# Expert weights prepared by ScalarE and VectorE beside the sampled scores, and VectorE's order in the recurrence changed

## The reference

```python
h = tok(x)                                        # splice, project, bias
u = layernorm(h)                                  # L0 attention: a complex linear recurrence
Bu = einsum(u, gamma * (B_re + 1j*B_im))
hs = scan(lambda s, b: s * lam + b, Bu)           # lam = exp(-exp(nu) + 1j*exp(theta)), 256 states
h += real(einsum(hs, C)) + einsum(u, D)
u = layernorm(h)                                  # L0 experts: 16, hidden 512, top 2
logits = u @ gate.T; top2; w = softmax(top2)
y_mean[e] = mean over e's tokens of silu(u @ w1[e].T), times w2[e]
h += sum over the 2 chosen of w * y_mean[e]
u = layernorm(h)                                  # L1 attention: 8 heads of 16, L = 166
q, k, v = u @ Wq, u @ Wk, u @ Wv
M = max - mean over 38 sampled keys of q . k      # "sampled scores"
top 25 queries by M attend to all keys, the others get mean(v)
h += out @ Wo
u = layernorm(h)                                  # L1 experts: 64, hidden 256, top 42
h += sum over e of comb[e] * (gelu(u @ w1[e] + b1[e]) @ w2[e] + b2[e])
```

## Time and profile before

| | us |
|---|---|
| median of 3 runs (2061.93 to 2066.79) | 2064.61 |
| the profiled execution | 2067.39 |
| its span (first to last instruction) | 2065.7 |
| recurrence, from the first outputs to the last routed group | 94 to 228 |
| last rows sent, PE idle | 228 to 283.3 |
| first experts, tiles | 283.3 to 397.7 |
| first experts, means and outputs | 397.7 to 429 |
| third norm, and start of the sampled scores | 429 to 465.9 |
| sampled scores, 16 chunks | 465.9 to 583.7 |
| attention of the chosen queries | 583.7 to 717 |
| fourth norm, routing and second experts | 717 to 2065.7 |

### The profile page before, as it was taken

The page is one execution under the profiler, slowest core; times in us unless marked ns, Lnnn a source line. Parts: engine busy times, 40 slices in busy tenths (PEclk is TensorE's granted clock), DMA queues, the critical chain, the costliest instruction groups (busy, mean ns, idle before and its releaser), DMA issues.

```text
span 2065.7 us, 50535 instructions
## 1 busy us (share of the span) xinstructions
PE 1870.1 (91%) x17038; PEld 1349.7 (65%) x17038; DVE 1676.4 (81%) x4833; ACT 1378.0 (67%) x2149; POOL 1455.0 (70%) x1098
## 2 busy tenths in 40 slices
PE   7887436789989978999999999999999999999998
PEld 5555213456669855777777777777777777777776
DVE  5887736555678788899999999999999999999998
ACT  4134525424435545888888888888888888888886
POOL 2216679559800032888888888888888888888887
PEclk9998768789989965999999999999999999999999
DMA  3011289523200010000000200000100000000000
GB/s 93 21 35 63 81 246 257 124 67 94 90 1 1 22 63 1 2 2 0 0 0 3 82 2 0 0 0 35 49 1 0 0 0 2 2 10 11 10 11 19
DMA packets 64334, 77.56 MB, mean 38 GB/s; under 512 B 38932, under 2 KB 47028, under 8 KB 62132
## 3 DMA queue, kind: packets, MB, share of 16 engines
q1 hardware_dynamic: 61364, 70.08, 11.7%
q0 software_dynamic: 2816, 5.45, 0.8%
HBM read 42.97 MB, written 24.08 MB: 32 GB/s over the span
## 4 chain that ended last, share of the span: by engine, by line
PE 58%; DVE 3%; issue 2%; ACT 1%; POOL 0%; ACTq 0%; DVEq 0%; POOLq 0%
PE bank L2679 30%; PE bank L2662 28%; DVE m_work L2553 1%; DVE m_best L2550 1%; DVE m_work L2544 0%; PE bank L2632 0%; DVE m_ut L1269 0%; ACT m_h L2485 0%; DVE m_best L2543 0%; DVE m_ex L2555 0%; DVE h L2591 0%; DVE m_red L2556 0%; DVE m_row L2536 0%; POOL m_diag L1255 0%; ACT m_hidden L2482 0%
## 5 line engine op out<-in xcount | busy, mean ns | idle before, releaser
L2679 PEld LDWEIGHTS bank<-weights,m_h 128*128 128x128 f16 x10752 | 649.6, 98 | 194.4 <-DVE hc L2582 82.6
L2430 POOL TENSOR_TENSOR m_h<-m_hidden,m_h 128x896 f16<-128x896 f32 x384 | 725.9, 1890 | 32.0
L2679 PE MATMUL bank<-weights,m_h 128*128 128x128 f16 x10752 | 724.6, 219 | 10.7 <-POOL m_h L2430 2.1
L2582 DVE SCALAR_TENSOR_TENSOR hc<-bank,m_shares,hc 128x128 f32<-128x128 f32 x2688 | 727.2, 342 | 4.3 <-PE bank L2679 4.3
L2482 ACT ACTIVATE m_hidden<-bank,m_b 128x896 f32<-128x896 f32 x384 | 386.9, 1007 | 197.6 <-PE bank L2662 197.5
L2567 DVE TENSOR_TENSOR m_h<-bank,m_h 128x896 f16<-128x896 f32 x384 | 419.2, 1092 | 116.8 <-ACT m_h L2485 116.7
L2428 POOL TENSOR_SCALAR m_h<-m_hidden 128x896 f16<-128x896 f32 x384 | 360.8, 939 | 117.9 <-ACT m_hidden L2482 99.5
L2662 PE MATMUL bank<-m_u_first,weights 128*128 128x448 f16 (+1 forms) x1536 | 417.8, 354 | 5.5 <-DVE h L2591 5.5
L2662 PE MATMUL bank<-m_u_second,weights 128*128 128x448 f16 (+1 forms) x1536 | 417.7, 354 | 0.0
L2479 ACT ACTIVATE bank<-bank,m_b 128x896 f32<-128x896 f32 x384 | 377.6, 983 | 0.6 <-PE bank L2662 0.6
L2485 ACT ACTIVATE m_h<-bank 128x896 f16<-128x896 f32 x384 | 349.1, 909 | 0.0
(11 more groups left out here) (359 smaller groups left out, 2153.9 us busy)
## 6 DMA issues: line engine op xcount, KB each, us to landing
weights<-expert_factors SPq DMA_DIRECT2D x12, 1024.0 KB, 8.8
lru_w_in<-e_w_dram SPq DMA_DIRECT2D x16, 512.0 KB, 4.5
expert_factors<-lru_w_out SPq DMA_DIRECT2D x16, 512.0 KB, 4.3
ew_raw<-e_w_dram SPq DMA_DIRECT2D x16, 512.0 KB, 3.9
weights<-w_dram SPq DMA_DIRECT2D x16, 256.0 KB, 2.8
weights<-w_dram SPq DMA_DIRECT2D x4, 1024.0 KB, 6.6
expert_factors<-ew_made SPq DMA_DIRECT2D x8, 512.0 KB, 3.0
xs<-x_dram SPq DMA_DIRECT2D x4, 996.0 KB, 11.8
```

Source lines behind the costliest of these rows:

```text
L2430: g.tensor_tensor(h1[:, x, 1], hidden[:, x], h1[:, x, 0], ALU.subtract).then_inc(second_of[1], 1)
L2582: last = v.scalar_tensor_tensor(acc[:, m * TW:(m + 1) * TW], y[q][:, (n - start) * TW:(n - start + 1) * TW], shares[:, m, e:e + 1], acc[:, ...
L2679: last = t.matmul(y[q][:, (n - start) * TW:(n - start + 1) * TW], factors[:, m, n * TW:(n + 1) * TW], k.weights[:, grp % 2, 2 + m, at], st ...
```

## The change

Four things are changed together.

1. Pieces are halved (`PIECES = 8`, 512 columns; 64 pieces, a group is 16). POOL makes pieces 0 to 31 (groups 0 and 1), none in the third norm, two per chunk behind `pool_diagonal` of chunks 1 to 15, and two behind the last.
2. The late pieces 32 to 63 (groups 2 and 3) move from the first experts into the sampled scores, two per chunk: ACT makes the rounded part and the scaled whole (`act_piece`, two instructions of 128x512 after the second and the fourth token-major copy), DVE one instruction (`dve_piece`, before the first and the third sampled score). They have a room of their own: 4 raw buffers, 4 made, 2 wide. The third norm's squares lie in the same room. SP's list of the block is one loop over chunks for both kinds.
3. The first experts' w2 is loaded whole before the tiles, ahead of the zero fills in SP's list, into four separate homes; between the transposing DMAs nothing is left. Every sixth set of SiLU is summed by ACT itself (two instructions with an accumulator in place of one, and no DVE instruction).
4. In the recurrence DVE makes the four additions first, with `dve_place` and `dve_rows` of the group before after the second, then `dve_weights`, then the four splits, and `state_part(g + 1, 1)` last.

```diff
@@ recurrence, sync @@
+            mixture.sync_second(sp, y_ready)
             routing.sync_fill(sp)
-            mixture.sync(sp, y_ready)
+            mixture.sync(sp)
@@ recurrence, gpsimd @@
             mixture.pool_clear(pool)
-            mixture.pool(pool)
@@ recurrence, vector @@
-                for i in range(2):
+                for i in range(STEP):
                     add(g, i)
-                    split(STEP * g + i)
                     if g == 0:
                         normed(2 * PERG + 2 * i)
                         normed(2 * PERG + 2 * i + 1)
+                    if g and i == 1:
+                        routing.dve_place(dve, g - 1)
+                        routing.dve_rows(dve, g - 1)
                 if g:
-                    routing.dve_place(dve, g - 1)
-                    routing.dve_rows(dve, g - 1)
                     routing.dve_weights(dve, g - 1)
+                for i in range(STEP):
+                    split(STEP * g + i)
                 if g + 1 < NGR:
                     state_part(g + 1, 1)
-                for i in range(2, STEP):
-                    add(g, i)
-                    split(STEP * g + i)
...
@@ FirstMixture @@
+    def sync_second(self, sp, outputs_made):
+        sp.wait_ge(outputs_made, NC)
+        sp.wait_ge(self.k.w0_split, NC)
+        for q in range(4):
+            self.sync_down(sp, q)
...
             sp.dma_start_transpose(self.xt[:, j % self.RING], k.slots[bass.ds(rows[j], ST), :]).then_inc(self.x_in[j % self.RING], 16)
-            if j in self.W2_AT:
-                self.sync_down(sp, 1 + self.W2_AT.index(j))
-            if j >= self.KEEP_FROM and (j - self.KEEP_FROM) % self.KEEP_EVERY in (0, 2):
-                late.sync_keep(sp)
...
+            if self.act_sums(j):
+                for f in range(self.FP):
+                    at = j % self.PARTS * self.FP + f
+                    last = self.nc.scalar.activation(self.set_banks(j)[:, f], self.set_banks(j)[:, f], ACT.Silu,
+                                                     accum_out=self.part[:, j // self.PARTS, at:at + 1])
@@ sparse_attention, sync @@
-                k.expert_weights.sync_pieces(sp, *PIECES_N3)
-                k.expert_weights.sync_pieces(sp, *PIECES_SAMPLE)
+                early, late = k.expert_weights, k.late_weights
+                for s in range(2):
+                    early.sync_load(sp, s)
+                sp.wait_ge(stats.var, NC + DEEP)
+                for i in range(4):
+                    late.sync_load(sp, i)
+                for c in range(NC):
+                    for s in range(2):
+                        late.sync_load(sp, 2 * c + 4 + s)
+                    for s in range(2):
+                        late.sync_keep(sp, 2 * c - 2 + s)
+                    for s in range(2):
+                        early.sync_keep(sp, 2 * c - 2 + s)
+                        early.sync_load(sp, 2 * c + 2 + s)
...
@@ sparse_attention, gpsimd @@
-                k.expert_weights.pool_pieces(pool, *PIECES_N3)
-                first, end = PIECES_SAMPLE
                 for c in range(NC):
                     norm.pool_diagonal(pool, c, c % 2, stats)
-                    if 1 <= c <= end - first:
-                        k.expert_weights.pool_pieces(pool, first + c - 1, first + c)
+                    if c:
+                        k.expert_weights.pool_pieces(pool, PER_CHUNK * (c - 1), PER_CHUNK * c)
+                k.expert_weights.pool_pieces(pool, PER_CHUNK * (NC - 1), PER_CHUNK * NC)
@@ LateWeights @@
     def sync_load(self, sp, i):
         if i >= self.count:
             return
...
+        if i >= 4:
+            sp.wait_ge(self.raw_read, i - 3)
...
+    def act_piece(self, act, c, j, s):
+        b = 2 * j + s
+        act.wait_ge(self.raw_in[b], 8 * c + 16 - 8 * j)
+        if not isinstance(c, int) or c >= 2:
+            act.wait_ge(self.kept_out[b], 8 * c - 8 * j)
+        self.nc.scalar.activation(self.made[:, b, 0], self.raw[:, b], ACT.Copy).then_inc(self.rounded, 1)
+        if not isinstance(c, int) or c:
+            act.wait_ge(self.split, 2 * c + s - 1)
+        self.nc.scalar.activation(self.wide[:, s], self.raw[:, b], ACT.Copy, scale=1.0 / SHARE).then_inc(self.raw_read, 1)
+
+    def dve_piece(self, dve, c, j, s):
+        b = 2 * j + s
+        dve.wait_ge(self.rounded, 2 * c + s + 1)
+        dve.wait_ge(self.raw_read, 2 * c + s + 1)
+        self.nc.vector.scalar_tensor_tensor(self.made[:, b, 1], self.made[:, b, 0], 1.0 - 1.0 / SHARE, self.wide[:, s], ALU.mult,
+                                            ALU.add).then_inc(self.split, 1)
```

143 lines of the change are left out of this document (66 added, 77 removed).

## The result

The changed kernel takes 2141.15 us (median of 4 runs, 2138.67 to 2142.22) against 2064.28 us (4 runs, 2061.93 to 2066.79): 1.037 times the time before, 95% interval 1.0353 to 1.0388. 2063 was predicted, with a range of 2040 to 2080. It is slower by 77 us, and the prediction was wrong.

What follows compares the result with a forecast made beforehand. It took DMA work to bound the first tiles and PE the sampled scores. Terms -1 - 44 - 1 - 8 + 50 + 4.5, another -2, gave about -2 in all: 2063 us on the median's scale, range 2040 to 2080.

Steps and rivals of the forecast that it cites:

- the chain of the sampled scores: Sampled scores: PE's chunk c - 1 through ACT, SP, load, POOL to chunk c + 1; 19.7 us against 14.7; +50.
- SP issues a load and two stores: Sampled scores, chain step: 0.38 us each and some 0.1 for the semaphore, 1.25 us, bringing the chain to 8.0.
- POOL's pair: Sampled scores, chain step: two half pieces and their eight starts take about 7.05 us, bringing the chain to 18.65.
- the loads' chain: Sampled scores: POOL's loads wait behind ACT's late piece, so PE waits about 5 us before every second spread, seven waits.
- The rival without it: Sampled scores: PE waits 4 to 5 us but returns to full clock at once; 2047 us, chance 0.20.
- the slower one: Sampled scores: PE's clock stays down through the chunk after each wait; 2080 us, chance 0.18.
- The tiles: First experts' tiles: DMA work lifted, ACT next at 4.63 us per six sets; 70 us instead of 114.4, -44.
- its row of PE's waits: First experts' tiles: PE's matmuls read as idle 74.5 us there, 60.0 of it for a transposing DMA.
- The recurrence: Recurrence: second rows two splits earlier, 1.2 us gained, a little lost to the additions; -1 us, bounds -3 and +4.
- the norm: Third norm: POOL's pieces leave, -5 for PE's diagonal wait and -3 for DVE, together -8; another -2 for PE's clock.
- The second experts,: Behind the sampled scores: nothing of the 1480 us changes.

Runs made afterwards that it cites:

- the groups alternating: Changed kernel, SP's order kept, POOL's pieces alternating between group 0 (not stored) and group 1 (stored): 2075.41 us, 1.0044 of before.
- the order alone: For the 98 us: changed kernel, SP's list in POOL's order, 2042.86 us. For the recurrence: kernel before with DVE's new order, 2062.08 us.
- PE's reads ahead: Changed kernel with PE's 43 expert numbers read into registers before the first tile, not at tiles 0, 16 and 32: 2131.85 us.
- the run with both edits: Changed kernel with SP's list in POOL's order, four homes for finished pieces (scaled copy in place), and POOL's last steps first: 2115.15 us, 1.0253 of before.

## Why the prediction was wrong

**The step that failed** is the chain of the sampled scores: "SP issues a load and two stores", with the landing of a load behind it, and "POOL's pair". It had the loads' chain and none of the stores of POOL's own pieces. Half of these pieces go to `kept` out of two homes, the cast of n waits for the store of n - 2, and the new list put that store behind ACT's piece of its own chunk. So from piece 18 on the chain is closed within one chunk (23.7 us by the trace) and not over two. This was to be read from the kernel: `ExpertWeights.sync_keep` stands beside `sync_load` in the list that I quoted, and the page of before gives its landing. I followed the buffer that is filled and not the one that is emptied. The experiments size it: with the groups alternating 66 us go, with the order alone 98. Of the 78.9 us that the stretch from the first spread to `attend` took over its forecast (133.4 for 54.5), 67.6 go with the alternating groups, and 11.3 are the loads' chain, priced too low.

**The loads' chain held, some 20% too short.** For the first half I forecast about 5 us before every second spread and 21.9 us for two chunks; the trace has 4.1, then 6.1 to 6.6, and 23.6. Where only this chain was left (alternating groups) the stretch grew by 65.8 us, to be set against 54.5 predicted. One of these chains, from the spread at 459.43 to that at 483.02:

```profile
467.54 0.63 ACT L2291 ACTIVATE lw_room<-lw_room 128x512 f32<-128x512 f32 x1
469.56 1.17 SPq L2208 DMA_DIRECT2D ew_raw<-e_w_dram  x2
474.30 0.61 POOL L2228 CAST weights<-ew_raw 128x512 f16<-128x512 f32 x1 [6.46 <-DMA ew_raw<-e_w_dram]
482.23 0.74 POOL L1251 TENSOR_TENSOR at_diag<-ident,rstd 128x332 f32<-128x332 f32 x1
```

ACT's second piece ends at +8.7 and not at 6.75, as ACT's first late piece stands between the copies and PE is at half clock, and SP issues the loads at +10.1 (forecast 8.0). The cast follows the issue by 4.7 us, where I took 3.6: the median landing was 4.2 us in this half and 4.2 for the alternating groups; the 3.1 of the whole kernel is lower by the loads of the second half. POOL's pair takes 7.9 us up to the diagonal, where I took 7.05. The prediction also names a fit of the Trainium skill, "DMA: Bandwidth & Descriptors" (section "Anatomy of one DMA"); the page gives it for DMAs issued by GpSimd, and these are issued by SP. The forecast's 3.6 did not come from it.

**The clock.** Each of PE's nine waits for a diagonal, 4.13 to 14.97 us long, has a spread of 1.45 to 1.48 us behind it, twice the 0.72 at full clock, as the rule of the Trainium skill, "TensorE: Matmul & The Clock Gate" (section "Part 1: The HAM clock gate"), says of half rate after idleness; the trace agrees. From the first spread to `attend` PE was busy 144.1 us, at a mean clock of 0.77, for work that took 124.0 before: 20 us. The rival without it was wrong, the slower one described part of what came but put its cause in the clock alone.

**The tiles.** -30.7 for -44. ACT is the bound and six sets take 4.7 us, close to the 4.63 worked out; with PE's reads ahead the stage takes 72.2 us, where the forecast was 70. The missing term is PE's reading of 16 and then 11 numbers into registers at tiles 16 and 32: 9.9 us of stops and the clock behind them. The trace of the kernel before shows the same two stops:

```profile
330.81 14.66 PE L1403 MATMUL bank<-lru_ut,weights 128*128 128x384 f16 x64 [5.58 <-issue]
370.96 9.81 PE L1403 MATMUL bank<-lru_ut,weights 128*128 128x384 f16 x40 [4.35 <-issue]
```

They could have been priced from there. That they cost nothing in the kernel before, where the DMA engines were 0.96 busy, is likely and was not tested. The prediction also read its row of PE's waits wrongly: of the 60.0 us for a transposing DMA, 36.04 lie ahead of the first tile, and only 24.0 within the 114.4 us. The conclusion that DMA work bound the stage did not hang on it: taking that work away brought 30.7 us. I costed what covers an edit, and not what the old bound had covered.

**The recurrence and the norm.** -3.5 for -1. POOL's third group of sends does start 3.4 us earlier, more than the two splits' 1.2 that I allowed, but the start of the tiles doesn't follow the sends: the order alone moves it by 1.0 to 1.6 us, as forecast, and the other 2 us or so come with the rest of the change, in the shorter time from the first zero fill to the first transposing DMA (26.7 us for 28.7). The traces show where they go: SP no longer issues two late loads and a load of w2 there (1.6 us), and the fills are issued in 11.5 us and not 12.0. The means, the norm and what is around it: -9.3 for -11. The wait of 4.96 us for the diagonal is gone, and DVE's two instructions of 83x38 take 0.51 us with POOL idle, not 2.43.

**The second experts,** -15.8 for nothing. Unchanged code, the same 102.5 us up to the first expert's matmul in both traces, then a loop that runs some 1.2% faster: in 200 us of it, before and after,

```profile
1020.00:1220.00 200.00, 198.73 (x2267) 144.73 (x2265) 182.24 (x503) 169.26 (x189) 177.76 (x127) 1.00 0.06 22
```

```profile
1110.00:1310.00 200.00, 200.00 (x2293) 144.90 (x2291) 185.00 (x511) 170.92 (x192) 179.95 (x128) 1.00 0.06 22
```

2267 matmuls against 2293. Before, the two tiles of an expert take 3.28 and 3.08 us in turn, and PE pauses 0.2 us in one of them; after, both take 3.11 to 3.16. The changed kernel and the eleven built on it have 1333 to 1336 us for this stretch, the two with the old parts (before, and the recurrence's order alone) 1348 to 1349. DVE's order upstream is excluded, and so are the buffers' addresses; what of the change sets the loop's rhythm is open. It is a fifth of the size of the loss, and no view of the kernel before foretells it. It is luck in the forecast's favour: without it the kernel would have missed the 2063 us by 94 us and not by 78.

## What to carry to other kernels

When the work of two producers is merged into one in-order list of DMAs, write down for each entry what it waits for and who waits for it, loads and stores alike; a wait at the head holds everything behind it, and the order of a few lines was worth 98 us here. A ring has two ends: follow the buffer that must be emptied as closely as the one that is filled. And when a bound is lifted, look for the stops that it had covered (here PE's register reads) and for the clock that they cost.

## What the runs showed that was not expected

- The time in which a store of 256 KB lands differs with what SP issued just ahead of it: POOL's stores took 2.3 and 2.2 us (medians) with POOL's order, 3.5 behind two late loads and two late stores, and 4.9 in the run with both edits, where SP issued seven DMAs within 4 us.
- PE's read of expert numbers into registers stops it for 5.7 us (16 numbers) and 4.2 us (11 numbers), some 0.36 to 0.38 us each, and the profile gives it to no engine ("issue").
- Two small DVE instructions of 83x38 took 2.43 us beside a working POOL and 0.51 us beside an idle one.
- The same loop, with the same code, runs in one of two rhythms 1.2% apart: one in all twelve profiles with the whole change, the other in the two with the old parts.
